# Folding the value and skip weights from rounded parts: twelve one-pass products in place of four full fp32 products per batch

## The chip, the cores and the metric

One core of one Trainium2 chip runs the whole kernel. The metric is the device time of one execution in microseconds (us), the median over several runs. Inside the core, TensorE (PE) multiplies matrices, VectorE (DVE), ScalarE (ACT) and GpSimd (POOL) do elementwise work, SyncE (SP) issues most of the transfers. The queue of an engine is served in order. "PEld" in the rows is TensorE's loading of weights, which the profile keeps apart from the matmuls (PE).

## The reference

Eight batches of 512 tokens by 256 features, 16 heads of 16. Cut to what matters:

```
x = x * s1;  x = (x - mean) / sqrt(var + eps)
q = (x @ Wq.T) * q_dc;  k = (x @ Wk.T) * k_dc          # *_dc: rsqrt(sum(W^2 * s^2) + eps), per batch
v_flat = (x @ Wv.T) * v_dc * s2                        # s1, s2: the two halves of cond, per batch
out  = softmax(q k^T / 4) v                            # per head
out  = (out @ Ww.T) * w_dc
skip = (v_flat @ Wu.T) * u_dc
z = out + skip
result = x_input + int8_quantised(z) @ int8_quantised(rhs) * scales
```

The skip term is two products in a row with a column scale between them: x Wv^T diag(v_dc s2) Wu^T. The kernel multiplies the two weights first, once a batch (the *fold*), so that one product of x with a 256x512 right side gives the value and the skip together.

## The kernel before

**Precision.** fp32r products take one pass of TensorE and keep fewer bits. The kernel gets precision back by splitting an operand in a high part (rounded to fp32r) and a low part (value minus high part, rounded too), and by summing three of the four products of parts (`PART_PRODUCTS`: high-high, high-low, low-high). Projections of q and k (line 1141) and values with skip (line 1164) are made so, with 512 columns a matmul. A plain fp32 matmul shows as two records on TensorE, each with its weight load; the fold (line 1152), the output product (line 1224), the transposes (line 1076) and the products of probabilities and values (line 1113) are plain fp32.

**The fold.** On GpSimd, `scale_values(a)` (lines 425 to 430) multiplies Wv by the batch's columns into `wv_scaled` and signals `wvs_ready`. On TensorE, `skip_matrix(a)` (lines 1144 to 1154) waits for that and makes four fp32 matmuls of 256 columns (eight records) into a PSUM bank. VectorE and ScalarE split the bank into high and low parts in `vs_w`, which `values` uses. `wu_t`, the transposed Wu, is copied out of PSUM once, by ScalarE (line 545).

**Order on TensorE.** It is written out by hand. Batch t is 8 steps; each step runs two rounds: `scores_of(r)` (four matmuls in two pairs, line 1099), the products with v of the two rounds before (two times eight records, line 1113), `scores_of(r + 1)`, and a fill, `fill(t, i)`, with work for the next or the last batch. The fold of batch t+1 is fill 6 of batch t for t = 0 to 6; from t = 2 on it stands behind an int product (`int_product`, line 1267, bf16, 256 columns, four matmuls). The second pair of scores of a round may start only when ScalarE has finished the exponentials (line 577) of the second pair of the round before, for there are two sets of score banks. In step 6 ScalarE also copies the accumulated output of the first two head groups (`save_first`, line 586), ahead of those exponentials. This copy is unmasked, GpSimd separates its halves (lines 465 and 466): both versions of the kernel have this.

**Order at the start.** TensorE: transposes of the weights, projections of batch 0, sums for the demodulation (line 1406), then

```
            pe.wait_ge(wu_ready, 1)
            keep_clock(norms_bank(0), 5)
            norms(0)
            skip_matrix(0)
            norms_transposed(0)
            rows_of_first()
            values(0, 0)
            row_maxima(0, USE[("v", 0, 0)] + 1)
```

and the loop over batches. `keep_clock` is matmuls whose results nobody reads. VectorE: `low_part(0, 0)`, `low_part(0, 1)`, `modulate(1)` (line 664), `sums(1, ...)` (line 915), a reciprocal (line 963), after which GpSimd runs `demodulation()` (lines 412 to 422) and `scale_values(0)`. SyncE: loads of the q and k stacks (line 298), the store of the demodulation rows to DRAM (line 340), then, for batch 1, a wait for that store and for `v_ready` of all four tiles of batch 0 (`v_and_skip`, line 724), and only then `load_rows` (line 265) and `load_x(2)` (lines 261 and 262), on which `modulate(2)` of VectorE waits; behind that stand in VectorE's queue the low parts of batch 1, for which TensorE's `norms(1)` (line 1172) waits.

Of the kernel before, what the change touches and what calls it, by code (L numbers as in the profile page):

```python
# [6 lines left out]
F32R = mybir.dt.float32r  # L7
BF16 = mybir.dt.bfloat16
I32 = mybir.dt.int32
ALU = mybir.AluOpType  # L10
# [3 lines left out]
P = 128  # L14
# [7 lines left out]
PART_PRODUCTS = ((0, 0), (0, 1), (1, 0))  # L22
# [42 lines left out]
def adaln_ffn_kernel(nc, x, cond, wq, wk, wv, ww, wu, rhs, out):  # L65
# [38 lines left out]
    with ctx:  # L104
        def sb(name, shape, dt=F32):
            return ctx.enter_context(nc.sbuf_tensor(name, shape, dt))

        def sem(name):
            return ctx.enter_context(nc.semaphore(name))
# [4 lines left out]
        half = sb("half", [P, 1])  # L114
        wv_nat = sb("wv_nat", [P, HC, H])
        ww_t = sb("ww_t", [P, HC, H])
        wu_t = sb("wu_t", [P, HC, H])
        table = sb("table", [P, 1])
        first_batch = sb("first_batch", [B, P])

        qk_w = sb("qk_w", [P, 2, 2, HC, H], F32R)
        vs_w = sb("vs_w", [P, 2, HC, 2 * H], F32R)
# [3 lines left out]
        rhs_inv = sb("rhs_inv", [P, HC])  # L126
        rhs_scale_row = sb("rhs_scale_row", [P, H])
        cond_t = sb("cond_t", [P, 2 * HC, B])
        cond_sq = sb("cond_sq", [P, 2 * HC, B])
        demod = sb("demod", [P, 5 * HC, B])  # L130
        demod_sum = sb("demod_sum", [P, 5 * HC, B])
        demod_t = sb("demod_t", [P, 5 * HC, B])
        cols = sb("cols", [P, B, 4])

        x_sb = sb("x_sb", [P, KT, H])
# [11 lines left out]
        bound = sb("bound", [1, 1])  # L147
        flag = sb("flag", [1, 1], I32)
        wv_scaled = sb("wv_scaled", [P, HC, H])
        w_demod = sb("w_demod", [P, 2, HC, H])  # L150
        skip = sb("skip", [P, 2, KT, H])
        v_aug = sb("v_aug", [P, KT, NH, DV])
# [22 lines left out]
        w_sq = probs_flat[:, 0:5 * HC * H].rearrange("p (m c i) -> p m c i", m=5, c=HC)  # L175
        zero_rows = probs_flat[0:2 * NP, 5 * HC * H:5 * HC * H + S]
        cond_nat = probs_flat[0:B, 5 * HC * H + S:5 * HC * H + S + 2 * H]

        y_q = sb("y_q", [P, KT, H])
        x_res = sb("x_res", [P, KT, H])  # L180
# [26 lines left out]
        def first_bank(m):  # L207

            return scores[:, m, :] if m < 4 else o_acc[:, :]
# [18 lines left out]
        cols_ready, demod_rows_ready = sem("cols_ready"), sem("demod_rows_ready")  # L228
        work_ready, work_freed = sem("work_ready"), sem("work_freed")
        wvs_ready, wd_ready = sem("wvs_ready"), sem("wd_ready")  # L230
        var_ready, rstd_ready, xn_ready, xt_ready = sem("var_ready"), sem("rstd_ready"), sem("xn_ready"), sem("xt_ready")
        hi_ready, low_ready, zero_stored = sem("hi_ready"), sem("low_ready"), sem("zero_stored")
        squares_ready, norms_summed, norms_ready = sem("squares_ready"), sem("norms_summed"), sem("norms_ready")
# [146 lines left out]
        def _(pool):  # L380
# [44 lines left out]
            def scale_values(a):  # L425

                for c in range(HC):
                    last = nc.gpsimd.tensor_scalar(wv_scaled[:, c, :], wv_nat[:, c, :], cols[:, a, 2 + c:3 + c],
                                                   None, ALU.mult)
                last.then_inc(wvs_ready, 1)  # L430

            def demodulate_output(b):

# [72 lines left out]
        def _(act):  # L506
# [14 lines left out]
            def rounded(m, dst, done):  # L521
                nc.scalar.activation(dst, first_bank(m).rearrange("p (c o) -> p c o", c=HC), ACT.Copy).then_inc(done, 1)
# [19 lines left out]
            rounded(WV, vs_w[:, 0, :, 0:H], split_hi)  # L542
            first_features(0)
            first_features(1)
            rounded(WU, wu_t[:, :, :], wu_ready)
            rounded(WW, ww_t[:, :, :], ww_ready)

            def high_part(a, n):
# [89 lines left out]
        def _(dve):  # L638
# [21 lines left out]
            def modulate(a):  # L660

                dve.wait_ge(x_loaded, a * 16)
                dve.wait_ge(style_loaded, a * 16 + 16)
                link(nc.vector.tensor_tensor(x_sb[:, :, :], x_sb[:, :, :],  # L664
                                             rows[:, 0, :].unsqueeze(1).broadcast_to([P, KT, H]), ALU.mult))
# [25 lines left out]
            def low_part(a, n):  # L691

                g = n // 2
                bank = scores[:, n, :] if a == 0 else ready("k" if n % 2 else "q", a, g)
                dve.wait_ge(hi_ready, a * 4 + (n + 1))
                if n % 2:
                    nc.vector.tensor_tensor(parts[:, n, 1, :], bank, parts[:, n, 0, :], ALU.subtract
                                            ).then_inc(low_ready, 1)
                else:
                    nc.vector.scalar_tensor_tensor(parts[:, n, 1, :], bank, cols[:, a, g:g + 1],  # L700
                                                   parts[:, n, 0, :], ALU.mult, ALU.subtract
                                                   ).then_inc(low_ready, 1)
                if a > 0:
                    dve.wait_ge(low_ready, a * 4 + (n + 1))
                    dve.sem_inc(work_freed, 1)
# [251 lines left out]
            dve.wait_ge(cols_ready, 1)  # L957
            low_part(0, 0)
            low_part(0, 1)
            modulate(1)  # L960
            sums(1, other_chunks)
            dve.wait_ge(root_ready, 2)
# [111 lines left out]
        def _(pe):  # L1074
# [69 lines left out]
            def skip_matrix(a):  # L1144

                pe.wait_ge(wvs_ready, a + 1)
                if a == 0:
                    pe.wait_ge(wu_ready, 1)
                bank = claim("fold", a, 0)
                for hc in range(HC):  # L1150
                    for c in range(HC):
                        last = nc.tensor.matmul(bank[:, hc * H:(hc + 1) * H], wv_scaled[:, c, hc * P:(hc + 1) * P],  # L1152
                                                wu_t[:, c, :], start=(c == 0), stop=(c == HC - 1))
                last.then_inc(work_ready, 1)

            def values(b, k):
# [275 lines left out]
            for n, ms in enumerate(((WV, WW), (WU,))):  # L1432
# [2 lines left out]
                    for g in range(HC):  # L1435
                        last = transpose(bank[0:B, i * H + g * P:i * H + (g + 1) * P], demod[:, m * HC + g, :])
                last.then_inc(work_ready, 1)
            pe.wait_ge(wu_ready, 1)
            keep_clock(norms_bank(0), 5)
            norms(0)  # L1440
            skip_matrix(0)
# [60 lines left out]
```

## Time and profile before

| | before |
|---|---|
| median of 3 runs | 421.37 us (419.68 to 421.5) |
| profiled execution, its own time | 420.03 us |
| span of its trace | 418.2 us |
| PE, ACT, DVE, POOL busy | 96%, 69%, 66%, 38% of the span |
| mean granted TensorE clock | 0.989 |

The profiled execution's time is 1.8 us more than its span. A busy share says how much of the span an engine had an instruction running, not whether that instruction held up the end; the chain that ended last says the latter.

### The profile page before, as it was taken

The page shows a single profiled execution, that of the slowest core. Times are in us where ns is not written, and L with a number is a line of the kernel's source. Part 1 is how long each engine was busy: PE and PEld are TensorE (multiplying, and loading weights), DVE is VectorE, ACT ScalarE, POOL GpSimd, SP SyncE. Part 2 cuts the span into 40 slices and gives each one's busy share as a digit, 9 for nine tenths or more (in the row PEclk, how much of TensorE's full clock was granted, in tenths as well). Part 3 has the DMA queues.
Part 4 walks back from the last instruction along what each step waited for, and adds up shares of the span by engine and source line. Part 5 has one row for each costly group of instructions (what it writes and reads, how often), then busy time and mean ns, then how long its engine had stood idle before and what let it go on. Part 6 is the DMA issues. An engine that isn't in the chain of part 4 may idle for free.

```text
span 418.2 us, 7636 instructions
## 1 busy us (share of the span) xinstructions
PE 401.9 (96%) x2542; PEld 215.0 (51%) x2542; DVE 275.2 (66%) x632; ACT 287.0 (69%) x327; POOL 157.2 (38%) x147
## 2 busy tenths in 40 slices
PE   8899898999999999999999999999999999998894
PEld 7785453455544455544545545454445544453363
DVE  7676387366856787467847787558847555648355
ACT  3526776767777687677775877667776787677811
POOL 7178062503460072705361172606370343341501
PEclk9889999999999999999999999999999999999998
DMA  5399627502873355721772365732772058502031
GB/s 161 120 136 132 140 54 139 119 29 88 136 128 86 100 100 129 184 96 50 133 175 62 101 112 129 173 101 54 136 169 77 17 129 137 142 0 103 1 102 50
DMA packets 29328, 44.20 MB, mean 106 GB/s; under 512 B 3880, under 2 KB 15144, under 8 KB 29256
## 3 DMA queue, kind: packets, MB, share of 16 engines
q1 hardware_dynamic: 27360, 38.84, 42.8%
q0 software_dynamic: 1040, 3.70, 2.8%
q10 hardware_dynamic: 880, 1.07, 1.4%
q8 instruction: 25, 0.41, 0.4%
q14 instruction: 23, 0.19, 0.2%
HBM read 14.17 MB, written 4.25 MB: 44 GB/s over the span
## 4 chain that ended last, share of the span: by engine, by line
PE 80%; DVE 7%; DMA 6%; issue 2%; SPq 2%; ACT 1%; ACTq 0%; DVEq 0%
PE o_acc L1113 26%; PE scores L1099 18%; PE work L1164 10%; PE work L1141 9%; PE work L1224 6%; PE work L1152 3%; DMA rows_dram<-o_n 2%; PE scores L1141 2%; DMA y_q<-in_L_cond_k_weight_dram 1%; PE work L1267 1%; SPq L298 1%; ACT probs L577 1%; DMA rows<-in_cond_dram 1%; DMA x_res<-in_L_cond_u_weight_dram 1%; PE work L1253 1%
## 5 line engine op out<-in xcount | busy, mean ns | idle before, releaser
L577 ACT ACTIVATE probs<-scores 128x1024 f32<-128x1024 f32 x256 | 247.7, 1023 | 77.0 <-PE scores L1099 74.3
L1113 PE MATMUL o_acc<-probs,v_aug 128*32 128x512 f32 x1024 | 123.1, 598 | 0.0
L1099 PE MATMUL scores<-q_stack,k_stack 50*128 50x512 f32 x512 | 95.8, 448 | 3.9 <-ACT probs L577 3.6
L1099 PEld LDWEIGHTS scores<-q_stack,k_stack 50*128 50x128 f32 x512 | 38.9, 184 | 75.1 <-ACT probs L577 60.6
L1113 PEld LDWEIGHTS o_acc<-probs,v_aug 128*32 128x32 f32 x1024 | 26.7, 109 | 60.6 <-issue 58.3
L402 POOL TENSOR_TENSOR rstd<-var_eps,half 128x4 f32<-128x4 f32 x8 | 8.6, 1079 | 115.0 <-DVE var_eps L676 112.6
L1164 PE MATMUL work<-vs_w,x_t 128*128 128x512 f32 x192 | 51.6, 410 | 0.2 <-DVEq L980 0.2
L465 POOL TENSOR_SCALAR den<-o_first,in_half 128x512 f32<-128x512 f32 x16 | 25.4, 1589 | 52.0 <-ACT o_first L586 51.8
L720 DVE TENSOR_TENSOR v_aug<-work,rows 128x128 f32<-128x128 f32 x64 | 15.6, 285 | 43.1 <-PE work L1164 42.5
L1141 PE MATMUL work<-x_t,qk_w 128*128 128x512 f32 x168 | 43.2, 405 | 0.0
L1164 PEld LDWEIGHTS work<-vs_w,x_t 128*128 128x128 f32 x192 | 34.2, 188 | 15.8 <-issue 7.6
L444 POOL TENSOR_TENSOR squares<-parts 128x512 bf16<-128x512 f32 x30 | 31.6, 1062 | 27.6 <-ACT parts L561 27.6
L452 POOL TENSOR_TENSOR res<-res,x_res 128x512 f32<-128x512 f32 x15 | 19.1, 1281 | 55.1 <-DVEq L866 55.1
L1141 PEld LDWEIGHTS work<-x_t,qk_w 128*128 128x128 f32 x168 | 30.4, 188 | 11.9 <-issue 4.8
L1224 PE MATMUL work<-w_demod,o_n 128*128 128x256 f32 x112 | 27.9, 392 | 0.0
L466 POOL TENSOR_SCALAR o_raw<-o_first,in_half 128x512 f32<-128x512 f32 x16 | 25.4, 1589 | 0.0
L1224 PEld LDWEIGHTS work<-w_demod,o_n 128*128 128x128 f32 x112 | 20.1, 189 | 7.3 <-issue 5.1
L779 DVE SCALAR_TENSOR_TENSOR den<-o_acc,in_half,den 128x512 f32<-128x512 f32 x16 | 12.0, 751 | 12.6 <-PE o_acc L1113 9.3
L664 DVE TENSOR_TENSOR x_sb<-x_sb,rows 128x1024 f32<-128x1024 f32 x7 | 8.9, 1273 | 15.1 <-DMA rows<-in_cond_dram 15.1
L816 DVE TENSOR_TENSOR y_q<-work,skip 128x512 f32<-128x512 f32 x16 | 11.0, 687 | 11.0 <-PE work L1224 10.1
L844 DVE TENSOR_SCALAR y_qt<-work 128x512 bf16<-128x512 f32 x14 | 9.7, 690 | 11.7 <-issue 10.0
L860 DVE SCALAR_TENSOR_TENSOR res<-work,y_scale,rhs_scale_row 128x256 f32<-128x256 f32 x28 | 12.2, 478 | 5.1 <-PE work L1267 3.6
(169 smaller groups left out, 458.9 us busy)
## 6 DMA issues: line engine op xcount, KB each, us to landing
q_stack<-parts SPq DMA_DIRECT2D x96, 128.0 KB, 3.9
k_stack<-parts SPq DMA_DIRECT2D x92, 128.0 KB, 4.0
x_res<-in_x_dram SPq DMA_DIRECT2D x8, 512.0 KB, 4.4
x_sb<-in_x_dram SPq DMA_DIRECT2D x7, 512.0 KB, 5.0
out_dram<-res POOLq DMA_DIRECT2D x7, 512.0 KB, 4.5
rows<-rows_dram SPq DMA_DIRECT2D x7, 384.0 KB, 4.0
rows<-in_cond_dram SPq DMA_DIRECT2D x8, 128.0 KB, 4.8
x_sb<-in_x_dram SPq DMA_DIRECT2D x2, 256.0 KB, 4.3
```

The costliest lines, as they stand in the source:

```text
L444: nc.gpsimd.tensor_tensor(squares[:, n, :], parts[:, n, 0, :], parts[:, n, 0, :], ALU.mult).then_inc(squares_ready, 1)
L452: nc.gpsimd.tensor_tensor(res[:, two, :], res[:, two, :], x_res[:, two, :], ALU.add).then_inc(res_added, 1)
L465: nc.gpsimd.tensor_scalar(den[:, :], o_first[:, :], in_half[:, 1:2], None, ALU.mult)
L466: nc.gpsimd.tensor_scalar(o_raw[:, :], o_first[:, :], in_half[:, 0:1], None, ALU.mult).then_inc(first_parted, 1)
L577: nc.scalar.activation(probs[:, r % RING, pair:pair + 2, :], scores[:, pair:pair + 2, :], ACT.Exp).then_inc(exp_done, 1)
L720: nc.vector.tensor_tensor(v_aug[:, k, :, e * D:(e + 1) * D].rearrange("p (n e j) d -> p n e j d", e=2, j=4)[:, :, e, :, :], both[:, 0:H].r ...
L1099: last = nc.tensor.matmul(scores[:, 2 * (u % 2) + e, :], k_stack[top:top + ROWS, t % 2, head, kt * P:(kt + 1) * P], q_stack[top:top + ROWS ...
L1113: last = nc.tensor.matmul(o_acc[DV * j:DV * (j + 1), :], v_aug[:, kt, 4 * g + j, :], probs[:, r % RING, 2 * (j % 2) + j // 2, :], start=(k ...
L1141: last = nc.tensor.matmul(bank, lhs, right, start=(n == 0), stop=(n == len(operands) - 1))
L1152: last = nc.tensor.matmul(bank[:, hc * H:(hc + 1) * H], wv_scaled[:, c, hc * P:(hc + 1) * P], wu_t[:, c, :], start=(c == 0), stop=(c == HC ...
L1164: last = nc.tensor.matmul(bank, lhs, right, start=(n == 0), stop=(n == len(operands) - 1))
L1224: last = nc.tensor.matmul(bank[:, k * H:(k + 1) * H], o_n[:, c, tok], w_demod[:, z % 2, c, :], start=(c == 0), stop=(c == HC - 1))
```

## The change

The fold is made from rounded parts too. `wu_t` becomes `wu_parts`: ScalarE writes the high part, and VectorE, between `low_part(0, 1)` and `modulate(1)`, writes the low part from PSUM (once). `scale_values` gains a copy of `wv_scaled` into the high part and a subtraction for the low part, both 128x512 on GpSimd, once a batch, with two waits of GpSimd on itself; `wvs_ready` comes after them. `skip_matrix` issues 12 fp32r matmuls of 256 columns in place of 4 fp32 ones (8 records). TensorE waits at the start for `wu_ready` of 2. Three small tiles (`first_batch`, `cond_sq`, `demod_t`) move into the space of `probs`, which is used for nothing else that early. The words that name the change also speak of an unmasked copy of the first head group; the diff has no line on it.

```
@@ (tiles)
-        wu_t = sb("wu_t", [P, HC, H])
+        wu_parts = sb("wu_parts", [P, 2, HC, H], F32R)
-        first_batch = sb("first_batch", [B, P])
-        cond_sq = sb("cond_sq", [P, 2 * HC, B])
-        demod_t = sb("demod_t", [P, 5 * HC, B])
+        wv_parts = sb("wv_parts", [P, 2, HC, H], F32R)
+        first_batch = probs_flat[0:B, 8 * S:8 * S + P]
+        demod_t = probs_flat[:, 9 * S:9 * S + 5 * HC * B].rearrange("p (c b) -> p c b", b=B)
+        cond_sq = probs_flat[:, 8 * S + P:8 * S + P + 2 * HC * B].rearrange("p (c b) -> p c b", b=B)
@@ (scale_values, GpSimd)
-                last.then_inc(wvs_ready, 1)
+                last.then_inc(wv_scaled_done, 1)
+                pool.wait_ge(wv_scaled_done, a + 1)
+                nc.gpsimd.tensor_copy(wv_parts[:, 0, :, :], wv_scaled[:, :, :]).then_inc(wv_high, 1)
+                pool.wait_ge(wv_high, a + 1)
+                nc.gpsimd.tensor_tensor(wv_parts[:, 1, :, :], wv_scaled[:, :, :], wv_parts[:, 0, :, :], ALU.subtract
+                                        ).then_inc(wvs_ready, 1)
@@ (ScalarE, start)
-            rounded(WU, wu_t[:, :, :], wu_ready)
+            rounded(WU, wu_parts[:, 0, :, :], wu_ready)
@@ (VectorE, start)
             low_part(0, 0)
             low_part(0, 1)
+            dve.wait_ge(wu_ready, 1)
+            nc.vector.tensor_tensor(wu_parts[:, 1, :, :], first_bank(WU).rearrange("p (c o) -> p c o", c=HC),
+                                    wu_parts[:, 0, :, :], ALU.subtract).then_inc(wu_ready, 1)
             modulate(1)
@@ (skip_matrix, TensorE)
                 if a == 0:
-                    pe.wait_ge(wu_ready, 1)
+                    pe.wait_ge(wu_ready, 2)
                 bank = claim("fold", a, 0)
                 for hc in range(HC):
-                    for c in range(HC):
-                        last = nc.tensor.matmul(bank[:, hc * H:(hc + 1) * H], wv_scaled[:, c, hc * P:(hc + 1) * P],
-                                                wu_t[:, c, :], start=(c == 0), stop=(c == HC - 1))
+                    operands = [(wv_parts[:, i, c, hc * P:(hc + 1) * P], wu_parts[:, j, c, :])
+                                for c in range(HC) for i, j in PART_PRODUCTS]
+                    for n, (lhs, right) in enumerate(operands):
+                        last = nc.tensor.matmul(bank[:, hc * H:(hc + 1) * H], lhs, right, start=(n == 0),
+                                                stop=(n == len(operands) - 1))
                 last.then_inc(work_ready, 1)
@@ (TensorE, start)
-            pe.wait_ge(wu_ready, 1)
+            pe.wait_ge(wu_ready, 2)
             keep_clock(norms_bank(0), 5)
```

## Rows read from the trace of the kernel before

**Rows 1.** The page: busy time by engine, and the chain that ended last.
```profile
PE 401.9 (96%) x2542; PEld 215.0 (51%) x2542; DVE 275.2 (66%) x632; ACT 287.0 (69%) x327; POOL 157.2 (38%) x147
...
PE 80%; DVE 7%; DMA 6%; issue 2%; SPq 2%; ACT 1%; ACTq 0%; DVEq 0%
```

**Rows 2.** Timeline, PE: start, duration, line, tiles, count; sums, projections, values.
```profile
20.52 2.81 PE L1406 MATMUL work<-cond_sq,probs 128*128 128x8 f32 x24
23.18 4.53 PE L1141 MATMUL scores<-x_t,qk_w 128*128 128x512 f32 x12
...
53.99 3.07 PE L1141 MATMUL work<-x_t,qk_w 128*128 128x512 f32 x12
...
134.36 1.67 PE L1164 MATMUL work<-vs_w,x_t 128*128 128x512 f32 x6
```

**Rows 3.** Groups by line and form: busy, mean ns of one.
```profile
L1152 PE MATMUL work<-wu_t,wv_scaled 128*128 128x256 f32 x64 | 15.4, 384 | 0.0
L1267 PE MATMUL work<-rhs_q,y_qt 128*128 128x256 bf16 x56 | 8.1, 274 | 0.0
...
L1164 PEld LDWEIGHTS work<-vs_w,x_t 128*128 128x128 f32 x192 | 34.2, 188 | 15.8 <-issue 7.6 <-DVEq L848 1.1 <-DVEq L980 0.6
```

**Rows 4.** Timeline, PE then ACT, around the fold of batch 3 (t = 2).
```profile
163.90 0.61 PE L1267 MATMUL work<-rhs_q,y_qt 128*128 128x256 bf16 x4
164.35 1.89 PE L1152 MATMUL work<-wu_t,wv_scaled 128*128 128x256 f32 x8
166.17 0.73 PE L1099 MATMUL scores<-q_stack,k_stack 50*128 50x512 f32 x4
166.83 1.92 PE L1113 MATMUL o_acc<-probs,v_aug 128*32 128x512 f32 x16
...
164.26 1.94 ACT L577 ACTIVATE probs<-scores 128x1024 f32<-128x1024 f32 x2 [0.18 <-ACT o_first L586]
```

**Rows 5.** Timeline, all engines, around the fold of batch 2 (t = 1).
```profile
117.87 2.00 PE L1152 MATMUL work<-wu_t,wv_scaled 128*128 128x256 f32 x8
...
118.22 1.94 ACT L577 ACTIVATE probs<-scores 128x1024 f32<-128x1024 f32 x2 [0.18 <-ACT o_first L586]
...
120.21 0.19 PEld L1099 LDWEIGHTS scores<-q_stack,k_stack 50*128 50x128 f32 x2 [0.24 <-ACT probs L577]
...
120.65 1.92 PE L1113 MATMUL o_acc<-probs,v_aug 128*32 128x512 f32 x16
```

**Rows 6.** Timeline, DVE, at the start.
```profile
17.64 0.69 DVE L910 TENSOR_TENSOR qk_w<-scores,qk_w 128x512 fp32r<-128x512 f32 x1 [0.24 <-DVE x_t L952]
18.25 0.68 DVE L910 TENSOR_TENSOR vs_w<-scores,vs_w 128x512 fp32r<-128x512 f32 x1
...
21.95 1.56 DVE L664 TENSOR_TENSOR x_sb<-x_sb,rows 128x1024 f32<-128x1024 f32 x1
23.54 0.21 DVE L915 TENSOR_SCALAR demod_sum<-work 128x48 f32<-128x48 f32 x1
```

**Rows 7.** Timeline, POOL, and POOL's groups by form.
```profile
26.75 1.87 POOL L428 TENSOR_SCALAR wv_scaled<-wv_nat,cols 128x256 f32<-128x256 f32 x2
...
L389 POOL CAST ident_b<-ident 128x128 bf16<-128x128 f32 x1 | 0.3, 279 | 0.0
...
L422 POOL COPY cols<-demod 128x16 f32<-128x16 f32 x1 | 0.2, 209 | 0.1
...
L452 POOL TENSOR_TENSOR res<-res,x_res 128x512 f32<-128x512 f32 x15 | 19.1, 1281 | 55.1 <-DVEq L866 55.1
...
L465 POOL TENSOR_SCALAR den<-o_first,in_half 128x512 f32<-128x512 f32 x16 | 25.4, 1589 | 52.0 <-ACT o_first L586 51.8
```

**Rows 8.** Timeline, PE, the fold of batch 0 and the first scores.
```profile
29.73 2.00 PE L1152 MATMUL work<-wu_t,wv_scaled 128*128 128x256 f32 x8
...
35.41 0.73 PE L1099 MATMUL scores<-q_stack,k_stack 50*128 50x512 f32 x4 [0.19 <-issue]
```

**Rows 9.** Timelines of DVE and SP, and the chain, from 36 us on.
```profile
45.27 0.41 DVE L724 TENSOR_TENSOR skip<-work,rows 128x256 f32<-128x256 f32 x1
...
36.84 9.30 DMA rows_dram<-o_n
...
46.46 0.35 SPq L265 DMA_DIRECT2D rows<-rows_dram  x1
```

**Rows 10.** Timeline, PE, norms of batch 1.
```profile
63.94 1.92 PE L1113 MATMUL o_acc<-probs,v_aug 128*32 128x512 f32 x16
66.64 0.40 PE L1172 MATMUL work<-squares,head_ones 128*32 128x512 bf16 x4 [0.78 <-DVEq L705]
```

**Rows 11.** The waits: who, for whom, us in total, times, longest.
```profile
POOL rstd L402 <- DVE var_eps L676: 112.6, 6, 22.2
```

**Rows 12.** Stretches: PE busy (count), granted clock, DMA share, GB/s.
```profile
20.00:23.10 3.10, 3.10 (x27) 0.99 0.73 216
23.10:26.40 3.30, 3.30 (x10) 0.50 1.08 128
```

More of the change, by code:

```diff
@@ L230, in adaln_ffn_kernel @@
         wvs_ready, wd_ready = sem("wvs_ready"), sem("wd_ready")
+        wv_scaled_done, wv_high = sem("wv_scaled_done"), sem("wv_high")
         var_ready, rstd_ready, xn_ready, xt_ready = sem("var_ready"), sem("rstd_ready"), sem("xn_ready"), sem("xt_ready")
```

## The prediction

> **What bounds the kernel now.** I read the page first: TensorE is busy for 96% of the span and makes 80% of the chain that ended last, while ACT, DVE and POOL are far below [rows 1]. So in the loop over batches a microsecond taken off TensorE's queue counts, unless the next wait of that queue gives it back. Then I read the groups by form for what one fold costs, the timelines around three of the eight folds, and the chain over the first 67 us, where TensorE is not alone on the path: DVE, a store to DRAM and SP's loads carry it up to `norms(1)` at 66.64, before which TensorE stands idle for 0.78 us [rows 10].
>
> **One fold on TensorE, before.** Durations of single matmuls overlap, so I go by the distance between starts. The eight records take 1.89 us with the last one's own length of about 0.38 in it: (1.89 - 0.38) / 7 = 0.216 us a record [rows 3, 4], 8 x 0.216 = 1.73 us a fold.
>
> **One fold after.** Twelve one-pass fp32r matmuls of 256 columns: the trace has none of that form. Nearest rows: fp32r of 512 columns, 12 in 3.07 us and 6 in 1.67, so (3.07 - 1.67) / 6 = 0.233 a matmul [rows 2]; bf16 of 256 columns, 4 in 0.61 with the last 0.27 long, so (0.61 - 0.27) / 3 = 0.11 [rows 3, 4]. Two bf16 matmuls' worth of columns would be 0.216 to 0.22, so an fp32r matmul costs some 0.015 more than its columns. Lower bound 0.11 (its columns alone), upper bound 0.188, the length of one of its weight loads [rows 3], if loads could not be hidden behind only 256 columns. I take 0.11 + 0.015 = 0.125, because the 0.233 of the 512-column row leaves hardly any room for an exposed load. 12 x 0.125 = 1.50, a saving of 0.23 us a fold.
>
> Does a page speak against this? The Trainium skill, "TensorE: Matmul & The Clock Gate", section "LDWEIGHTS (loading the stationary operand)", gives a load of 128 columns 128 / 1.2 = 107 ns, and its section on the mechanism of packing says that loads overlap running matmuls only when they lie in another group of rows, which full 128-row weights never do. Taken at its word, an estimate by that page is 0.11 + 0.107 = 0.217 a matmul and 2.6 us a fold, 0.87 slower instead of 0.23 faster. By that rule the 512-column matmuls would stand some 0.32 apart; the trace has 0.233, so it does not bear the rule out here.
>
> **How much of it the loop keeps.** Batches t = 2 to 6: behind the fold come scores, whose second pair needs the end of the exponentials, at 164.26 + 1.94 = 166.20; the products with v start at 166.83, 0.63 later [rows 4]. At t = 1 the same distance is 120.65 - (118.22 + 1.94) = 0.49, and there the second pair did wait for ScalarE, 0.24 us by the row of its weight load [rows 5]. So 0.49 is the floor, and 0.63 - 0.49 = 0.14, say 0.15 with what rounding hides, is all that this step can give: of the 0.23 the rest turns into a wait for ScalarE. 5 x 0.15 = 0.75 us. At t = 1, and at t = 0, where no int product stands ahead either, the step already ends on that wait: gain 0.
>
> **GpSimd in the loop.** Added a batch: a copy of 128x512 and a subtraction of 128x512. The copy: from 16 elements in 0.209 to 128 in 0.279 is 0.6 ns an element, hence 0.52 at 512; the upper bound is the 1.59 of the scalar product of that size. The subtraction as the addition of `add_residual`, 1.28. With two gaps of some 0.08 that is 2.0 us (up to 3.0) [rows 7]. It costs nothing from batch 1 on: `scale_values` runs a whole batch before its fold, and GpSimd then stands idle before `inverse_root`, 112.6 us in 6 waits, 18.8 each [rows 11]. Without that cover `part_first` would be 2 us late, and with it VectorE's `add_second`.
>
> **The start.** Here nothing covers it. VectorE's new subtraction from PSUM is like line 910, which moves the next start by 18.25 - 17.64 = 0.61 us; `modulate(1)` ends at 23.51 and the sums start at 23.54, right behind it, so everything up to `scale_values(0)` is 0.61 late [rows 6]. That ends at 28.62 now [rows 7], then at 29.23, plus 2.0 of new work: `wvs_ready` at 31.2 and the fold at about 31.3 in place of 29.73, 1.55 us late. Behind it on TensorE stand the transposed norms, `rows_of_first`, `values(0, 0)` and the first scores, and for them DVE waits. Less the 0.23 that the fold is shorter by, all are 1.3 us late (scores at 36.7 instead of 35.41) [rows 8]. The flag of batch 0 comes late too, but before SP asks.
>
> How much survives? SP issues `load_rows` at 46.46, after the store of the rows (36.84 + 9.30 = 46.14) and after `v_and_skip(0, 3)`, which ends at 45.68 [rows 9]. That one moves to 47.0, and SP issues at about 47.15: 0.7 late. From there DVE's queue runs without slack up to the low parts of batch 1, so `norms(1)` is 0.7 late. TensorE itself comes there at 65.86 + 1.3 = 67.16, before 66.64 + 0.7 = 67.34: its idle time takes in the difference [rows 10]. Cost of the start: 0.7 us. Bounds: 0.2 (copy and subtraction at their quickest, DVE's subtraction half hidden) to 1.7 (copy at 1.59, nothing absorbed ahead of SP). The moved small tiles cost 0: same instructions, same waits, and `probs` is first written at the first exponentials. The twelve matmuls read one tile more, with no transfer.
>
> **Sum**, against the profiled execution's own 420.03 us: + 0.7 - 0.75 = - 0.05, 419.98. The median of the runs lies 1.34 above the profiled execution, so 421.3 for the median. Less than 0.5% (2.1 us) can't be told from no change in this kernel.
>
> **Rivals.**
> A. *The weight loads show.* At 0.188 a matmul a fold takes 2.26, 0.53 more. t = 2 to 6: 5 x 0.53 = 2.65. t = 0 and 1: 1.92 + 0.53 + 0.66 to the products with v, 3.11 against 2.78, 2 x 0.33 = 0.66. Start: TensorE 1.55 + 0.53 late, SP 1.4. Together + 4.7: 426.0. For it: each load record is 188 ns long; against it: the 0.233. It decides (over 2.1 us) from 0.160 a matmul on. Chance 7%.
> B. *Loads are never hidden.* 24 matmuls of only 8 columns take 2.81 us, 0.11 apart, nearly all of it weight load [rows 2]; each fp32r matmul would stand 0.11 + 0.11 = 0.22 apart, 2.64 a fold, 0.91 more; 5 x 0.91 + 2 x 0.71 + 1.8 at the start = + 7.8: 429.1. Against it the 0.233, in which 0.22 for the columns and 0.11 for the load don't fit. Chance 3%. This is how the rule of the Trainium skill's page named above would act.
> C. *The wait ahead of the fold lowers the clock.* TensorE would stand idle from 29.8 to 31.3. The granted clock fell to 0.50, the 1.2 GHz level, at 23.1 behind a stretch of 8-column matmuls, and 12 projections took 4.53 us there instead of 3.07 [rows 2, 12]. The same behind the new idle stretch would make `values(0, 0)` and the first scores 1.4 later: SP 2.1 late instead of 0.7, 422.7. For it: that stretch has no keep-clock matmuls; against: the fold itself runs in it. Chance 28%.
> D. *The start absorbs all* and the loop gives 0.75, or ScalarE's floor is lower than I read it and all 0.23 come through (1.15): 420.2 to 420.6. Chance 12%.
> The forecast itself: 50%.
>
> A and B give slower by over 0.5%, 10%, and C with noise of the medians another 2%: 12%. Faster by over 0.5% needs more than any case gives, only noise: 5%. Within: 83%. Range 419.4 to 423.6: D with the spread of the runs shown below, C with it above; A and B are left out.
>
> **What would show it.** Fold: 12 records, starts 0.125 apart. At t = 2 to 6 the step from int product to products with v 0.15 shorter, with the second pair's weight load now waiting for ScalarE. At the start: fold at 31.3, scores at 36.7, SP's `load_rows` at 47.15, `norms(1)` at 67.3. Two new rows on GpSimd, 0.5 and 1.3 us, and no new wait for `wvs_ready` after the first. The prediction is wrong if a matmul stands more than 0.16 apart, if a clock of 0.5 shows between 30 and 37 us, or if `inverse_root` on GpSimd becomes late.

## The result, and the profile after

The change makes the kernel slower. In 19 executions of each kernel the median goes from 420.47 us (419.54 to 422.46) to 424.54 us (420.65 to 428.42). The ratio, 1.0074 with a 95% interval of 1.0054 to 1.0095, is not the quotient of the two medians (1.0097): here and below a ratio leaves out the executions that lie more than 1.5% above the fastest of their kernel, here two of the changed kernel (427.49 and 428.42 us). The spread is a result too: it was 2.9 us and is now 7.8. The best execution of the changed kernel is 1.1 us slower than the best before and about as fast as the old median; the larger part of what it lost is no fixed cost but something that hits some executions more than others.

The profiled execution of the changed kernel took 425.84 us. The page, to be read against [rows 1] (busy time, two transfer queues, the chain):

```profile
span 424.0 us, 7717 instructions
...
PE 401.7 (95%) x2574; PEld 215.1 (51%) x2574; DVE 276.1 (65%) x633; ACT 286.9 (68%) x327; POOL 172.4 (41%) x163
...
q1 hardware_dynamic: 27360, 38.84, 48.9%
...
q8 instruction: 25, 0.41, 0.5%
...
PE 77%; DVE 7%; DMA 6%; issue 3%; ACT 3%; SPq 2%; ACTq 0%; DVEq 0%
```

TensorE is busy for 0.2 us less than before, while the span is 5.8 us longer: the time went into idle stretches of TensorE, not into its work. The fold itself is as predicted. The timeline of PE and POOL at the start (answers to [rows 7, 8]):

```profile
29.47 0.61 POOL L434 CAST wv_parts<-wv_scaled 128x512 fp32r<-128x512 f32 x1
...
30.16 1.26 POOL L436 TENSOR_TENSOR wv_parts<-wv_scaled,wv_parts 128x512 fp32r<-128x512 f32 x1
...
31.48 1.68 PE L1164 MATMUL work<-wu_parts,wv_parts 128*128 128x256 f32 x12 [1.49 <-POOL wv_parts L436]
...
36.75 0.49 PE L1109 MATMUL scores<-q_stack,k_stack 50*128 50x512 f32 x2
```

Twelve records in 1.68 us with the last about 0.27 long (the length of a matmul of 256 columns in [rows 3]) stand (1.68 - 0.27) / 11 = 0.128 us apart. And the step at t = 2 (answers to [rows 4]; PE, the load of the second score pair, and ACT):

```profile
166.53 0.61 PE L1279 MATMUL work<-rhs_q,y_qt 128*128 128x256 bf16 x4
...
166.89 1.94 ACT L584 ACTIVATE probs<-scores 128x1024 f32<-128x1024 f32 x2 [0.18 <-ACT o_first L593]
166.90 1.67 PE L1164 MATMUL work<-wu_parts,wv_parts 128*128 128x256 f32 x12
...
168.88 0.19 PEld L1109 LDWEIGHTS scores<-q_stack,k_stack 50*128 50x128 f32 x2 [0.20 <-ACT probs L584]
...
169.32 1.06 PE L1123 MATMUL o_acc<-probs,v_aug 128*32 128x512 f32 x8
```

From the int product to the products with v it was 2.93 us and is now 169.32 - 166.53 = 2.79; the exponentials end at 168.83 and the products start 0.49 later, on the floor, and the load of the second pair now waits for ScalarE. That is the 0.15 a fold, and the reason why it isn't 0.23.

Where do 5.8 us come from then? I laid the exponentials of the two traces beside each other, one by one, and noted by how much those of the changed kernel start later. A table of these distances (worked out from the two timelines; first and last exponentials of each batch t):

```
t        0     1     2     3     4     5     6     7
first  1.33  1.27  1.31  2.49  2.45  2.30  4.18  5.64
last   1.26  1.28  2.47  2.45  2.30  4.17  5.64  5.80
```

The start costs 1.33. At t = 2 to 6 each fold gives 0.15 back (in the table the other movements of the same batch hide part of it). And in the first steps of t = 2, 5 and 6 the distance leaps by 1.29, 2.13 and 1.60 us: 5.0 together, more than the whole loss of the medians. The timeline of PE there:

```profile
126.97 1.92 PE L1123 MATMUL o_acc<-probs,v_aug 128*32 128x512 f32 x14
...
129.14 1.04 PE L1123 MATMUL o_acc<-probs,v_aug 128*32 128x512 f32 x2 [0.26 <-issue]
...
268.43 0.50 PE L1109 MATMUL scores<-q_stack,k_stack 50*128 50x512 f32 x1
270.58 0.73 PE L1109 MATMUL scores<-q_stack,k_stack 50*128 50x512 f32 x3 [1.65 <-issue]
...
316.82 0.51 PE L1109 MATMUL scores<-q_stack,k_stack 50*128 50x512 f32 x2
...
318.67 0.50 PE L1109 MATMUL scores<-q_stack,k_stack 50*128 50x512 f32 x2 [1.34 <-ACT probs L584]
```

TensorE stops after 14 of 16 records, after one of four matmuls, and between the two pairs of scores. "issue" says that it waited for nothing that the profile shows, and the middle of a group has no semaphore to wait for. The third row names ACT, but those exponentials had ended at 316.79, 1.88 us before. What does stand next to each stop is a transfer of queue q8, 16 KB each. That this queue carries TensorE's instructions shows in two kernels further down: with 240 instructions more a batch in TensorE's code it makes 33 transfers (a_else240), with TensorE's unexecuted branch left out 21 (a_nobranch), in place of 25. The queues' shares in the 1.5 us up to the end of the middle transfer, and in the 1.7 us behind it, in which TensorE stands still and q8 has no transfer at all (267.3 to 268.8, and 268.8 to 270.5):

```profile
q1 hardware_dynamic: 123, 0.21, 104.4%
q8 instruction: 1, 0.02, 6.0%
...
q1 hardware_dynamic: 82, 0.15, 60.3%
```

The three q8 transfers begin at 125.8, 267.34 and 315.46 and end at about 127.5, 268.78 and 317.04; TensorE goes on 1.6 to 1.8 us after each end. Each comes with the start of a batch. There TensorE reads a flag and jumps over `row_maxima`'s unexecuted branch (64 matmuls, 4 transposes, their waits). The Trainium skill, "Runtime: NRT & Kernel Launch", section "Instruction fetch mechanics", says that a sequencer refills a FIFO of instructions in blocks of 16 KiB over a queue of its own, mostly hidden, and that a taken branch to a page that isn't there must fetch it before execution goes on. By that rule the trace agrees in place and kind: stops only behind the jump. The profiled execution of before has the same jumps and 25 transfers on q8 too, and no such stop. That alone shows a neighbourhood and no cause. So I had three suspects for the stops and the spread (what the change does to the placement of tiles, GpSimd in the loop, the jump itself) and one for the rest (the start).

### The profile page after: what moved, and what is told of

The parts are those of the page before. It is cut to its first block, busy times and chain, and to the rows that moved or that the text cites. A ratio compares the mean times of both kernels' runs of the same rounds, so it can differ in the third digit from the quotient of the medians.

```text
span 424.0 us, 7717 instructions
## 1 busy us (share of the span) xinstructions
PE 401.7 (95%) x2574; PEld 215.1 (51%) x2574; DVE 276.1 (65%) x633; ACT 286.9 (68%) x327; POOL 172.4 (41%) x163
## 3 DMA queue, kind: packets, MB, share of 16 engines
q1 hardware_dynamic: 27360, 38.84, 48.9%
## 4 chain that ended last, share of the span: by engine, by line
PE 77%; DVE 7%; DMA 6%; issue 3%; ACT 3%; SPq 2%; ACTq 0%; DVEq 0%
PE o_acc L1123 26%; PE scores L1109 18%; PE work L1176 10%; PE work L1151 9%; PE work L1236 6%; DMA rows_dram<-o_n 3%; ACT probs L584 2%; PE scores L1151 2%; PE work L1164 2%; DMA y_q<-in_L_cond_k_weight_dram 2%; PE work L1279 1%; DMA rows<-in_cond_dram 1%; SPq L300 1%; DMA x_res<-in_L_cond_u_weight_dram 1%; PE work L1265 1%
## 5 line engine op out<-in xcount | busy, mean ns | idle before, releaser
L1109 PE MATMUL scores<-q_stack,k_stack 50*128 50x512 f32 x512 | 97.7, 451 | 7.2 <-ACT probs L584 5.4
L404 POOL TENSOR_TENSOR rstd<-var_eps,half 128x4 f32<-128x4 f32 x8 | 8.3, 1041 | 105.2 <-DVE var_eps L683 102.7
```

The costliest lines, as they stand in the source:

```text
L1109: last = nc.tensor.matmul(scores[:, 2 * (u % 2) + e, :], k_stack[top:top + ROWS, t % 2, head, kt * P:(kt + 1) * P], q_stack[top:top + ROWS ...
```

## The experiments

Each kernel was timed in 6 to 12 executions beside the kernel before, whose medians there lay between 420.65 and 421.45. They ran in five groups, on three chips, and the changed kernel was not timed again in them. So kernels of different groups are compared by their ratios to the kernel before, and a difference of two ratios carries the uncertainty of both, mostly some 0.3%; "give or take" below is that. The medians are those of all executions.

**Placement of the tiles.** q1's share rose from 42.8% to 48.9% with the same 38.84 MB. The new tiles had moved the q and k stacks by 64 bytes from a multiple of 512 bytes a partition. Two kernels shift the stacks of the kernel before, one puts those of the changed kernel back.

```
b_q64 (b_q128: 32 and 96), ahead of the stacks and behind them:
+        pad_a = sb("pad_a", [P, 16])
...
+        pad_b = sb("pad_b", [P, 112])
a_q512, ahead of the stacks; the first two stood behind them:
+        row_max = sb("row_max", [P, KT, NH])
+        inv_den = sb("inv_den", [P, S // DV, 2])
+        pad_a = sb("pad_a", [P, 16])
```

> The kernel before, with 64 bytes of padding ahead of q_stack and k_stack (and 448 behind them, so that all else keeps its place within 512 bytes). Theory placement: the changed kernel lost its time because its tiles moved by a number of bytes that is no multiple of 512 (the stacks from 0 to 64 within 512), and the 2 KB packets of the stack loads take longer at such a place: 206 ns in the mean instead of 171. Then this kernel, with nothing else of the change, has that too, its scores wait at the starts of some batches, and it comes to 423 to 425 us. Rival GpSimd: the two added passes on GpSimd slow the transfers; then this kernel is at 420.5, packets at 171 ns. Rival chance: the profile of the changed kernel caught a slow moment; then nothing changes either.

> The same with 128 bytes ahead of the stacks. If what counts is whether the start is a multiple of 128, the time is that of before (420.5) and the packets are at 171 ns; if it is a multiple of 512, it is as slow as with 64 bytes. Rivals GpSimd and chance: as before.

> The changed kernel whole, with two small tiles and 64 bytes of padding put ahead of the stacks, so that they start at a multiple of 512 as before. Theory placement: 2 KB packets near 171 ns, no waits at the starts of batches, 1.3 us lost at the start and 5 x 0.15 won in the folds: 421.0. Rival GpSimd and rival chance: as the changed kernel, 424.5 or a draw around it.

Measured: b_q64 421.89 us, ratio 1.0005 (0.9982 to 1.0028); b_q128 422.31, 1.0015 (0.9990 to 1.0039); a_q512 425.22, 1.0068 (1.0036 to 1.0100). In b_q64 q1's share is 45.9%: the placement does slow the packets, and by itself that costs nothing that can be measured here. The page of a_q512, transfers and time to landing (the changed kernel has 48.9% and 4.2):

```profile
q1 hardware_dynamic: 27360, 38.84, 43.0%
...
q_stack<-parts SPq DMA_DIRECT2D x96, 128.0 KB, 3.9
```

The packets are quick again and the kernel is as slow as it was. The theory fell.

**GpSimd in the loop.** b_pool is the kernel before with the copy and the subtraction of `scale_values` added and read by nobody; a_nopool is the changed kernel with both only for batch 0 (the folds of batches 1 to 7 then use the parts of batch 0).

```
a_nopool, in scale_values:
+                if a > 0:
+                    pool.wait_ge(wv_scaled_done, a + 1)
+                    pool.sem_inc(wv_high, 1)
+                    pool.sem_inc(wvs_ready, 1)
+                    return
```

> The kernel before with only GpSimd's part of the change: the copy and the subtraction in every batch, wvs_ready behind them; the fold stays fp32 and the stacks stay where they were. Theory placement: the start is later by about 0.8 us (GpSimd's 1.9 us less what SyncE and VectorE take in), nothing else: 421.2, packets at 171 ns. Rival GpSimd: the packets are slow here, 206 ns, and the time is 424 or more.

> The changed kernel without the copy and the subtraction on GpSimd from batch 1 on: the parts of the scaled weights are those of batch 0 in all eight folds. TensorE's code is that of the changed kernel. Theory fetch: as the changed kernel, 424 to 425. Rival GpSimd: 421.0.

Measured: b_pool 422.32, 1.0028 (0.9998 to 1.0058); a_nopool 426.73, 1.0145 (1.0112 to 1.0178). Without GpSimd's work in the loop the changed kernel isn't quicker, and its profile still has two stops, so that theory fell as well. (That it is slower than the changed kernel, clear of both intervals, I can't explain.) The trace of b_pool says the same more sharply: its exponentials are 2.93 us late in every round from t = 1 to the middle of t = 5, so GpSimd's two passes cost the loop nothing. b_pool is GpSimd's part of the late start, without VectorE's subtraction, about 1.2 us, and its interval reaches down to zero. Its profile also shows rival C at work. The timeline of PE, and the stretch from 30 to 34 us with the granted clock behind the busy times:

```profile
31.44 3.54 PE L1159 MATMUL work<-wu_t,wv_scaled 128*128 128x256 f32 x8 [2.33 <-POOL wv_parts L436]
...
38.62 0.49 PE L1106 MATMUL scores<-q_stack,k_stack 50*128 50x512 f32 x2
...
30.00:34.00 4.00, 2.56 (x7) 2.06 (x8) 0.51 (x1) 0.00 (x0) 3.91 (x4) 0.72 1.08 129
```

The eight records take 3.54 us in place of 2.00. A fall to the 1.2 GHz level (a granted clock of 0.50) came behind TensorE's wait for `wvs_ready` in 5 of the 9 profiles of kernels in which that fold starts late, and in none of the 11 in which it doesn't. It goes with how long TensorE stood idle there: 2.13 to 2.86 us in the five profiles with a fall (b_pool, a_q512, a_nobranch, a_else240, a_once128), 1.49 to 2.02 us in the four without (the changed kernel, a_m8, a_m16, a_nopool).

**The unexecuted code.** If the stops are the jump's, the code that is jumped over should matter, though none of it runs. These kernels add or take instructions there and change nothing else.

```
b_else16, and with their own numbers in place of the 16 b_else8, a_else240 and a_once128 (batch 0 only), in the Else of row_maxima:
+                    for _ in range(16):
+                        pe.sem_inc(spare, 1)
a_m16 (a_m8: NW + 16), same place, leaves out every second wait of 32:
-                            if n >= NW:
+                            if NW < n <= NW + 32:
+                                if (n - NW) % 2:
+                                    pe.wait_ge(m_freed, a * M_USES + (n - NW + 2))
+                            elif n >= NW:
```

> The kernel before with 16 semaphore instructions added on TensorE inside the branch that is never taken (row_maxima, once a batch). They are not executed; they only move all of TensorE's later code by as much as I count for the 12 matmuls in place of 4 (24 instructions for 8). Theory fetch: the stalls of the changed kernel, 1.3 to 2 us behind the jump over that branch, are waits for code, and whether they come depends on where the code lies; this kernel then comes to 422 to 425 us and its profile shows stalls on TensorE at starts of batches, put down to issue, next to a late transfer of the instruction queue. Rival GpSimd: the added passes on GpSimd cause them; then 420.5 to 421.2, no such stalls.

> The kernel before with 8 instructions more in the branch that is never taken. Placement theory: the stalls of the changed kernel without its start and without its gain, 423 to 425. Rival: 421.

> The changed kernel with 240 such instructions in the branch that is never taken: with the 16 of the change 256 a batch, a whole 16 KB of code, so that all the later code lies within its 16 KB block as before. Theory fetch: stalls gone, 421.0 (1.3 lost at the start, 0.75 won in the folds). If the number that counts is another, the time is another draw, 421 to 426. Rival GpSimd: 424.5.

> The changed kernel with 128 instructions (half of a 16 KB block) more in the branch of batch 0 alone, so that all later code moves by half a block. Placement theory: where a block ended shortly behind the landing of a jump it now ends half a block later, the stalls go: 421 to 422.5. Rival: 424.5.

> The changed kernel with 16 waits fewer in TensorE's branch that is never taken (the waits for freed banks are taken two at a time there), so that a batch of TensorE's code is as long as before. Theory of two costs (code placement in the loop, GpSimd's work at the start): no stalls behind the jumps, 0.15 won in each of five folds, 1.3 us lost at the start, and some 1.5 more of it in the executions in which the clock falls at the first fold: 421 to 422. If placement is not what sets the stalls: as the changed kernel, 424.5.

> The changed kernel with 8 waits fewer in the branch that is never taken: by the count of four instructions for an fp32 matmul and two for an fp32r one, each batch of TensorE's code is as long as before and each jump lands where it did. Placement theory: no stalls at starts of batches, 421 to 422.5 (the start's cost stays). Rival (placement is not it, something else in the loop): 424 to 425.6 like its neighbours.

Measured: a_else240 474.29 us, 1.1252 (1.1193 to 1.1310); a_once128 431.27, 1.0235 (1.0201 to 1.0269); b_else16 423.21, 1.0051 (1.0023 to 1.0079); b_else8 420.79, 1.0004 (0.9984 to 1.0024); a_m16 425.56, 1.0134 (1.0093 to 1.0175); a_m8 424.44, 1.0079 (1.0047 to 1.0112). Code that never runs costs up to 50 us, the falls of the clock behind its stops included (a_else240's mean granted clock is 0.942, the changed kernel's 0.996). The chain of a_else240, pieces that are idle without a cause, and PE's timeline at one of them:

```profile
39.34 10.70 issue
...
143.10 2.25 issue
...
246.94 3.81 issue
...
352.60 4.24 issue
```

```profile
140.51 1.66 PE L1176 MATMUL work<-vs_w,x_t 128*128 128x512 f32 x6
145.35 0.58 PE L1267 MATMUL work<-ident_b,y_int 128*128 128x128 bf16 x4 [3.18 <-issue]
```

With a longer branch the chain has such a piece at seven of the eight batches, 10.7 us at the first and 2.3 to 4.2 at the others. So unexecuted code can make such stops, and the nearest account of the changed kernel's own is the fetching of code. But it is not simply the length. a_m8, by the count of instructions as long per batch as the kernel before, has the changed kernel's time (its profile, taken in the fastest of its executions, 421.08 us, has no stop), and b_else8, with the length of the changed one, has the time of the kernel before. a_once128 has its long stop at batch 0 and none in the first steps of the other batches. a_m16 comes out slower than the changed kernel, not faster. And b_else16, 0.5% slower than the kernel before, has no stop behind a jump in its profile but two falls of the clock, so its loss is not shown to be one of fetching.

**Without the jump.** `row_maxima` on TensorE is left out: the flag isn't read and the case in which row maxima are needed is missing.

```
-                small = pe.value_load(flag[0:1, 0:1], min_val=0, max_val=1)
-                with pe.If(small == 1):
-                    pe.sem_inc(m_ready, M_USES)
-                with pe.Else():
...
+                pe.sem_inc(m_ready, M_USES)
```

> The changed kernel without the branch on TensorE: the case in which the row maxima are needed is left out there, and TensorE signals m_ready always. Nothing is jumped over. Theory fetch: no stalls, 420 to 421, and a narrow spread of the runs. Rival GpSimd: stalls and spread stay, 424.5.

> The kernel before without the branch on TensorE (the case in which the row maxima are needed is left out there). If the kernel before pays for the jumps too, in small waits or in some of its executions, it is faster than before: 418 to 420. If its jumps cost nothing, 421.0.

Measured: a_nobranch 422.78, 1.0029 (1.0002 to 1.0056); b_nobranch 421.32, 1.0019 (0.9992 to 1.0046). By the ratios, taking the jump out gives the changed kernel 0.45% back (1.9 us, give or take 0.34%) and the kernel before nothing that can be measured. Without the jump in both, the change costs 0.10% (give or take 0.38%), into which the predicted - 0.05 us fits; with it, 0.74%. The edit takes out more than the jump: the reading of the flag goes too, and with the branch 4 of q8's 25 transfers. No run here separates the three, and "the jump" below stands for all of them. a_nobranch's trace has no stop in the loop; its span, 421.3, carries rival C in full. Windows of it from 34 on, and PE's timeline:

```profile
34.00:37.00 3.00, 3.00 (x6) 1.16 (x4) 2.05 (x6) 2.08 (x3) 3.00 (x2) 0.50 1.13 131
37.00:40.00 3.00, 3.00 (x9) 1.89 (x8) 0.44 (x2) 0.00 (x0) 3.00 (x2) 0.50 1.06 124
```

```profile
37.07 2.93 PE L1176 MATMUL work<-vs_w,x_t 128*128 128x512 f32 x6
39.93 0.54 PE L1109 MATMUL scores<-q_stack,k_stack 50*128 50x512 f32 x2
...
70.61 0.40 PE L1184 MATMUL work<-squares,head_ones 128*32 128x512 bf16 x4 [0.28 <-DVEq L712]
```

Scores 3.2 us later than in the changed kernel's own profile (36.75), and `norms(1)` at 70.61 in place of 67.89.

**The start as before.** a_start makes the fold of batch 0 in fp32 from a copy of Wu that ScalarE makes ahead of the high part, without GpSimd's two steps, and moves VectorE's subtraction behind the low parts of batch 0. a_best and a_best8 do that and take 16 or 8 instructions out of the branch (a_best8 from batch 1 on).

```
-                    operands = [(wv_parts[:, i, c, hc * P:(hc + 1) * P], wu_parts[:, j, c, :])
-                                for c in range(HC) for i, j in PART_PRODUCTS]
+                    if a == 0:
+                        operands = [(wv_scaled[:, c, hc * P:(hc + 1) * P], wu_first[:, c, :]) for c in range(HC)]
+                    else:
+                        operands = [(wv_parts[:, i, c, hc * P:(hc + 1) * P], wu_parts[:, j, c, :])
+                                    for c in range(HC) for i, j in PART_PRODUCTS]
```

> The changed kernel with the fold of batch 0 as before (fp32, from a copy of Wu in space of the probabilities), GpSimd's two passes from batch 1 on alone, and VectorE's subtraction moved from ahead of modulate(1) to behind low_part(0, 3). Theory of two costs: the start is that of before and the stalls stay: 0.75 won, 2 to 3 lost, 421.5 to 423, some 1.5 to 2 under the changed kernel. If the start costs nothing: 424.5.

> Both together. Theory of two costs: neither is paid, what is left is the 0.75 us won in the folds: 420.3, or 0.998 of before. If a third cost is in the change, it shows here: 421 or more.

> The changed kernel with the start as before and the branch shortened by 8 from batch 1 on. Placement theory: 420.3, the 0.75 us of the folds ahead of the kernel before. Rival: 422.9 like the version with 16.

Measured: a_start 423.37, 1.0047 (1.0020 to 1.0073); a_best 422.88, 1.0069 (1.0036 to 1.0102); a_best8 422.38, 1.0035 (1.0007 to 1.0063), with 4 of 12 executions at 420.1 to 420.6 and others up to 425. The start is worth 0.27% (1.1 us, give or take 0.33%, so alone not clear of noise). Something larger is left, and the shorter branches did not remove it.

**Both, and the placement with them.** a_startnb is a_start without the jump; a_all8 is a_best8 with the stacks back at a multiple of 512 bytes.

> The changed kernel with the fold of batch 0 in fp32 as before the change (so the start has its old length) and with the row-maxima case left out on TensorE, so that its code has no jump. Theory of two costs (the late start, and the jump at each batch's start): both are gone, only the saving of 0.15 us at five folds is left: 420.0 to 420.5 us, with a spread of the runs as narrow as that of the kernel before, and no wait named issue over 0.5 us at the start of a batch. Rival, a third cost that is in neither: 421.5 us or more.

> The kernel with the fold of batch 0 as before and eight instructions fewer in the unexecuted branch, and besides both the stacks and the tiles of parts placed so that the q and k stacks begin at a multiple of 512 bytes a partition, as before the change. If slow transfers of the stacks make the code behind the jump arrive late, both the stalls and the spread go: 420.3 us. If the placement has no part in it, this is as the same kernel without the placement was: 422.4 us, with single stalls at batch starts.

Measured: a_startnb 421.35 (420.52 to 423.72), 1.0006 (0.9986 to 1.0025); a_all8 421.30 (419.47 to 423.24), 0.9995 (0.9968 to 1.0022). With start and jump both undone the loss is gone: 0.27% and 0.45% taken from 0.74% leave 0.02%, measured 0.06%. The step from a_start to a_startnb is a second measurement of the jump, 0.41% (give or take 0.33%). The gain of the folds does not show, though: 0.75 us would be a ratio of 0.9982, just below the interval of a_startnb, so some 0.24% (1.0 us) is unaccounted for, and a third cost is not ruled out. Against b_nobranch (1.0019), the kernel before without the jump, a_startnb is 0.13% ahead, which fits the gain but lies within the noise. a_all8 came out 0.4% below a_best8, with intervals that overlap, and its trace still has a stop behind a jump, at 222.38 (idle 1.42 us). That placement matters together with the jump is therefore suggested and not shown.

## Why the prediction was wrong

I said 421.3 and no measurable change; it was 424.54, 0.74% slower, outside my range. The kernel before came out at 420.47 in these executions, 0.9 below the 421.37 I had started from, so by luck the absolute number misses by less than the change does. Point by point:

- **One fold: right.** 0.125 a matmul, measured 0.128. Weight loads are hidden behind 256 columns; rivals A and B didn't happen.
- **What the loop keeps: right.** 0.15 at each of five folds, 0 at t = 1, stopped by ScalarE's floor of 0.49.
- **GpSimd in the loop: right.** 0.61 and 1.26 us against 0.52 and 1.28; `rstd` still waits, 102.7 us in six waits, and the constant distance in b_pool's loop shows that this work costs nothing there.
- **The start: right up to the scores** (fold 31.48 against 31.3, scores 36.75 against 36.7, `v_and_skip(0, 3)` at 47.04 against 47.0). Then "SP issues at about 47.15: 0.7 late" failed. I held the landing of the store at 46.14 because it had taken 9.30 us [rows 9]. In the changed kernel it took 10.78 and stayed the later of SP's two waits, where I had put `v_and_skip(0, 3)`; with the start as before it took 11.34. The chain of the changed kernel, then of a_startnb:

```profile
36.81 10.78 DMA rows_dram<-o_n
...
47.91 0.35 SPq L267
```

```profile
36.15 11.34 DMA rows_dram<-o_n
```

  So the start cost 1.25 us at `norms(1)` in this profile, part of it not due to the change: of the eleven profiles whose chain shows the store, the 9.30 of the kernel before is the shortest (9.97 to 11.34 in the others). Over all profiles `norms(1)` starts at 66.36 to 68.85 where the first fold is early (eleven, the middle one 67.34), at 67.58 to 68.51 where it is late and the clock holds (four), and at 69.38 to 70.61 where the clock falls (three; the two kernels with long unexecuted code are left out, as a stop comes between). Without a fall the late start thus costs about 0.5, near my 0.7; the 1.1 of the ratios (a_start) is that with the falls averaged in.
- **Rival C: the right mechanism, in some executions, in one of them at too low a price.** The changed kernel's own profile kept the full clock between 30 and 37 us; b_pool, a_q512 and a_nobranch did not. I priced `values(0, 0)` and the first scores, 1.4 us; in a_nobranch the rows of the first batch ran at the low level too, and the scores came 3.2 later than in the changed kernel, `norms(1)` 2.7. I treated C as a case that holds or doesn't; the idle time ahead of the fold varies between executions, and the fall with it, so C belongs in the spread as well as in the sum.
- **The sum: this is the step that failed.** "+ 0.7 - 0.75 = - 0.05" held that outside the costed edits nothing moves. The stops of TensorE behind its jumps have no term there and no rival. They took 5.0 us of the changed kernel's profile, and what goes with the jump is worth 1.9 us by the ratios (a_nobranch against the changed kernel; 1.7 for a_startnb against a_start). With 1.1 for the start and 1.9 for the jump the sum becomes + 2.25, against the 3.1 us that 0.74% is; the rest, 0.85, is within the noise of these ratios and is not explained. That such stops exist could be read only in part: [rows 1] give 2% to "issue", and no such stop stands behind a jump of the kernel before. That a jump at each batch's start makes the timing depend on where code is fetched I could have named as a rival.

**What stays open.** Why do the same jumps stall the changed kernel and not the one before? Of the profiles of kernels with the jump (without the two long branches), none of six with the old fold loses more than 1 us in the first steps of any batch (one loses 0.67 once, b_else8), and five of nine with the new fold do, nine times together (the changed kernel 3, a_q512 2, a_nopool 2, a_m16 and a_all8 1 each). It is not the length of the code per batch by itself (the times of a_m8 and b_else8), not GpSimd (a_nopool), not placement alone (a_q512). Nor is it simply how late the transfer comes: in b_q128 one on q8 began at 266.35, 1.41 us after the first exponentials of its batch (t = 5), later than any of the changed kernel's three (1.00 us before, 0.88 and 0.61 after), and nothing stopped. Where a block ends in relation to what TensorE still has to do I can't see in these traces, and I have no run that sets it. With one profile of each kernel, and stops in five of nine, a single profile without a stop says little either: of the changed fold without the jump there are two, both without a stop.

A second thing varies too: in some executions the clock falls in the loop, mostly behind short waits for ScalarE. PE's timeline of a_best8 and its window from 72 to 75 us:

```profile
71.68 3.38 PE L1130 MATMUL o_acc<-probs,v_aug 128*32 128x512 f32 x16
...
72.00:75.00 3.00, 3.00 (x18) 0.40 (x10) 1.08 (x4) 0.86 (x1) 0.00 (x0) 0.56 0.85 131
```

Sixteen records in 3.38 us in place of 1.92, about 1.5 us lost at once. I found such falls in b_else16 (two), a_start (two), a_best8, a_startnb, a_nopool and a_m16, so with the old fold and with the new, and in the profile of neither kernel of the change. In a_q512 a fall came behind one of the stops at a jump (idle 1.35 us at 318.17; the 12 matmuls of `values` behind it took 4.61 us in place of 3.07), so a stop can cost its idle time and a fall besides. The falls widen every spread here, and one profile doesn't tell a median.

## What to carry to other kernels

A saving on the busiest engine is worth only what the next wait of its queue leaves: read the distance to that wait first (here 0.15 of 0.23). A cost at the start, where nothing covers, needs the chance of a clock fall behind the new idle time, and the variation of the transfers beside it, not one execution's row. Where a busy engine's queue has a jump, a change of its instructions may cost more than its own work does, here 0.74% with the jump and 0.10% without it; compare with the jump taken out before blaming the edit.

## What the runs showed of the hardware

- An fp32r matmul of 256 columns stands 0.128 us behind the one before, with a 128x128 weight load of 0.188 for each: less than one load's length (the changed kernel's profile).
- Unexecuted instructions on TensorE can cost time when they are jumped over: 240 more a batch (a_else240) 50 us in all, 128 once (a_once128) 6.7 us, both against the changed kernel's median and with the falls of the clock behind the stops; 8 more a batch (b_else8) nothing measurable.
- Behind a jump TensorE may stand still until 1.4 to 1.8 us after a 16 KB transfer of its code has ended, also in the middle of a group of matmuls (nine stops in five profiles; the kernel before has the same jumps and no stop).
- Ahead of the first fold, TensorE's idle times of 2.13 to 2.86 us were followed by a granted clock of 0.50 (five profiles), those of 1.49 to 2.02 us were not (four profiles).
- Moving the destination tiles of the stack transfers by 64 bytes a partition raised q1's share from 42.8% to 45.9% for the same bytes (b_q64), and the kernel's time not measurably (ratio 0.9982 to 1.0028).
- The same small store to DRAM took from 9.3 to 11.3 us to land in different executions, with and without the change.
